# Four fp32 load buffers instead of five, and five fp16 split buffers instead of four, in a graph network kernel

## The reference

```python
def L0(x, adj):                 # passes 1 to 4
    h = relu(adj @ (f1[:, None] * (adj @ (x @ W1))))
    return adj @ (f2[:, None] * (adj @ (h @ W2)))
def L1(x, adj):                 # pass 5
    return concatenate([x, adj @ x], 1) @ weight
def L2(x, adj):                 # pass 6, the gated one
    m = x @ W_msg + b_msg
    gates = sigmoid((m @ W_q) @ (m @ W_k).T / sqrt(128) + gate_bias) * adj * adj
    return layernorm_affine(relu(concatenate([x, gates @ m], 1) @ W_upd + b_upd))
def L3(x, adj):                 # passes 7 and 8
    x1 = swish((adj @ x) @ W + b)
    return swish((adj @ x1) @ W + b)
x = layernorm(x + L(x, adj))    # for L in L0, L1, L2, L3
```

## Time and profile before

| what | value |
|---|---|
| median of 3 runs | 1719.76 us (1717.48 to 1719.78) |
| the profiled execution's own time | 1721.57 us |
| its span, first to last instruction | 1719.7 us |
| mean granted TensorE clock | 0.984 |
| TensorE matmul busy | 1627.4 us (95%) |
| VectorE busy | 1289.4 us (75%) |
| ScalarE busy | 1087.7 us (63%) |
| moved by DMA | 473.99 MB, 276 GB/s over the span |

### The profile page before, as it was taken

How to read it: one execution, slowest core, us unless ns; L and a number is a source line. 1 busy time by engine, 2 the same in 40 slices (tenths; PEclk the granted TensorE clock), 3 DMA queues, 4 the chain that set the end, 5 groups by cost and what they waited for, 6 DMA issues and landing times. The chain is left out here.

```text
span 1719.7 us, 18856 instructions
## 1 busy us (share of the span) xinstructions
PE 1627.4 (95%) x7618; PEld 763.6 (44%) x7618; DVE 1289.4 (75%) x1439; ACT 1087.7 (63%) x741; POOL 11.3 (1%) x25
## 2 busy tenths in 40 slices
PE   7999999999999999999999999898998799999996
PEld 4444444444444444444454444343434344444442
DVE  6875547554766497749996898989899996455997
ACT  5766747674664566456666786776768666445653
POOL 2000000000000000000000000000000000000000
PEclk9999999999999999999999999999999999999998
DMA  9989889987997788668686454444445797665992
GB/s 366 410 297 399 299 354 388 374 305 301 367 356 278 265 319 325 263 245 317 248 298 261 147 205 162 171 171 171 171 172 194 295 365 284 250 236 198 345 340 109
DMA packets 66120, 473.99 MB, mean 276 GB/s; under 512 B 7568, under 2 KB 7728, under 8 KB 9072
## 3 DMA queue, kind: packets, MB, share of 16 engines
q1 hardware_dynamic: 64800, 468.22, 72.0%
q0 software_dynamic: 1088, 4.49, 0.7%
q10 hardware_dynamic: 144, 0.07, 0.0%
HBM read 420.32 MB, written 52.43 MB: 275 GB/s over the span
## 5 line engine op out<-in xcount | busy, mean ns | idle before, releaser
L928 DVE SCALAR_TENSOR_TENSOR a_lo<-a_ring,a_hi 128x2048 f16<-128x2048 f32 x332 | 752.2, 2287 | 306.8 <-ACT a_hi L726 306.5
L726 ACT ACTIVATE a_hi<-a_ring 128x2048 f16<-128x2048 f32 x332 | 629.9, 1906 | 359.9 <-PE spare L548 217.5
L548 PE MATMUL acc<-a_hi,y_hi 128*128 128x512 f16 x1584 | 480.6, 385 | 54.2 <-DVE a_lo L928 34.3
L548 PE MATMUL acc<-a_hi,y_lo 128*128 128x512 f16 x1584 | 477.2, 382 | 0.0
L548 PE MATMUL acc<-a_lo,y_hi 128*128 128x512 f16 x1584 | 477.2, 382 | 0.0
L548 PEld LDWEIGHTS acc<-a_hi,y_hi 128*128 128x128 f16 x1584 | 153.6, 99 | 249.9 <-DVE a_lo L928 41.7
L548 PEld LDWEIGHTS acc<-a_lo,y_hi 128*128 128x128 f16 x1584 | 156.4, 99 | 192.7 <-issue 10.0
L548 PEld LDWEIGHTS acc<-a_hi,y_lo 128*128 128x128 f16 x1584 | 155.8, 98 | 190.3 <-issue 5.7
L962 DVE SCALAR_TENSOR_TENSOR gates<-gates,a_ring 128x1024 f32<-128x1024 f32 x128 | 155.8, 1218 | 28.4 <-ACT gates L761 27.4
L946 DVE TENSOR_TENSOR a_lo<-gates,a_hi 128x1024 f16<-128x1024 f32 x128 | 155.8, 1217 | 0.0
L740 ACT ACTIVATE a_hi<-gates 128x1024 f16<-128x1024 f32 x112 | 118.0, 1054 | 56.5 <-DVE gates L962 56.2
(11 more groups left out here) (100 smaller groups left out, 718.4 us busy)
## 6 DMA issues: line engine op xcount, KB each, us to landing
a_ring<-adj_dram SPq DMA_DIRECT2D x348, 1024.0 KB, 7.0
saved_squares<-squares SPq DMA_DIRECT2D x48, 1024.0 KB, 11.7
a_ring<-saved_squares SPq DMA_DIRECT2D x48, 1024.0 KB, 4.8
x_T<-xt_dram SPq DMA_DIRECT2D x4, 512.0 KB, 8.2
x_rows<-x_dram POOLq DMA_DIRECT2D x1, 2048.0 KB, 12.7
out_dram<-x_rows POOLq DMA_DIRECT2D x3, 512.0 KB, 4.1
out_dram<-x_rows SPq DMA_DIRECT2D x2, 256.0 KB, 2.0
w<-W_dram POOLq DMA_DIRECT2D x2, 64.0 KB, 5.4
```

What stands on the lines that cost most here:

```text
L548: mm = pe.matmul(sums[:, h * BANK:(h + 1) * BANK], blk(y[:, y_pass % 2, :], j), slot(a, st)[:, s, h * BANK:(h + 1) * BANK], start=(begins ...
L726: act.activation(slot(a_hi, st), loaded(st), ACT.Copy, scale=2.0 ** A_EXP).then_inc(s_ahi, 1)
L928: dve.scalar_tensor_tensor(out=slot(a_lo, st).rearrange("p s c -> p (s c)"), in0=loaded(st).rearrange("p s c -> p (s c)"), scalar=2.0 ** A ...
```

## The change

Two constants are exchanged. One load buffer and one slot of both split rings have 8 KiB in each partition, so the memory is the same. Nothing else is edited, but all code that uses the constants follows: the wait of each load, the slots, the wait of `a_hi`, the position of every epilogue piece of the plain passes on ScalarE and VectorE, and the wait of GpSimd's small loads.

```diff
-LOADS = 5
-RING = 4
+LOADS = 4
+RING = 5
```

## The result

The changed kernel takes 1739.2 us (median of 4 runs, 1737.5 to 1739.7) beside 1719.8 before: ratio 1.0104, 95% interval 1.0092 to 1.0116. It is slower, as forecast, but by 19.4 us where 8 were forecast, and it lies 2 us above the upper end of the range. The profiled execution spans 1735.7 us, 16.0 more than before; the traces account for these 16.0, and the 3.4 us to the medians' difference are not in them. The profiled execution was the fastest of the four (1737.5 us, mean granted clock 0.979); the other three had a clock of 0.976 or 0.977.

What follows compares the result with a forecast made beforehand. TensorE was taken as the bound, with VectorE in layer-norm stretches and loads from 50 to 75 us. Terms summed to +7.95 us, 1729.5 against the profiled 1721.57, hence a median of 1727.7 us; range 1714 to 1737.

Steps and rivals of the forecast that it cites:

- the first claim under buffering: Buffering sum stays nine, so with PE as the bound a load starts at the same moment; only splits move.
- the loads starve: Rival: four buffers give 2.9 us a step at a 7.4 us landing, 25 to 30 us slower, 1747; chance 0.1.
- start: PE's first wait for y_lo, chunk 1: it stands behind the fifth split, +2.5 us, bounds 0 and 4.2.
- pass 2, 280 us: z_T at 279.00 behind one more a_hi and square: +3.5 us, bounds 1.2 and 5.5.
- pass 3, 454 us: z_T behind one more split, loads lying ready, so 1.5 us won back: +2.1 us, bounds 1.0 and 3.6.
- pass 4, first norm: First layer norm: wait of 3.42 us shrinks, but z_T comes later; +1.5 us, bounds -2.7 and 3.2.
- pass 4, 704 us: Extra split fits before the norm, closing PE's 2.49 us gap and its clock fall: -4.2 us.
- pass 5: Gap at 777.61 closes, z_T near 804 stands behind one more load: +0.3 us net, bounds -4.2 and +4.
- pass 7: VectorE saturated, last y_lo behind one more split, first loads a gated step later: +2.0 us, bounds -1.75 and 3.3.
- pass 8: Last norm's 2.59 us gap closes, about 1 us lost at a swish: -1.5 us, bounds -4.3 and +1.
- clock: One clock fall more, net of new and closed PE gaps: +1.75 us, bounds -1.75 and 5.2.
- The bursts decide: Rival: extra splits done in VectorE's idle time, pieces not late, gains stand alone: 8.9 us faster, 1711; chance 0.16.

Runs made afterwards that it cites:

- four loads alone: Kernel before with LOADS = 4 in place of 5 and RING kept at 4: 1735.8 us, ratio 1.0086.
- the half loads: Changed kernel with each load after the first four, except the gated pass's, cut to its first 0.5 MiB: 1720.6 us, ratio 1.0002.
- the old places: Epilogue pieces placed among the splits as before the change (`freed` with RING = 4); the changed kernel with them: 1739.2 us, ratio 1.0104.
- the new places: Epilogue pieces placed one split later, as by `freed` with RING = 5; put alone into the kernel before (five loads, four slots): 1821.2 us, ratio 1.0579.
- five and five: Kernel before with five load buffers, five split slots, three square slots: 1725.1 us (1.0024) with new places, 1714.3 us (0.9958) with old places.
- the control: Kernel before with three slots for the squares in place of four, k's low part overwriting its high part: 1721.4 us, ratio 1.0000.

## Why the prediction was right in sign and wrong in size

**The step that failed** is the first claim under buffering, that with nine steps kept the lost load buffer costs nothing, together with the case against "the loads starve". That a load starts at the same moment did hold: the issue of each load, less TensorE's own shift at that time, moved by 0.0 us in the median of the 57 loads from 30 to 230 us and by 0.7 in the 48 from 230 to 440. But a split that is one slot further ahead wants its load one step sooner. From issue to that moment there were 5 x 2.6 - 4.2 = 8.8 us before and are 4 x 2.6 - 4.2 = 6.2 us now (an estimate from the step and the split), and the landing takes 6.6 us in the median. Between 258 and 275 us ScalarE does this in the kernel before, then in the changed one:

```profile
262.47 1.91 ACT L726 ACTIVATE a_hi<-a_ring 128x2048 f16<-128x2048 f32 x1 [0.68 <-PE acc L548]
265.06 1.91 ACT L726 ACTIVATE a_hi<-a_ring 128x2048 f16<-128x2048 f32 x1 [0.68 <-PE acc L548]
```

```profile
266.18 1.91 ACT L726 ACTIVATE a_hi<-a_ring 128x2048 f16<-128x2048 f32 x1 [1.23 <-DMA a_ring<-adj_dram]
269.92 1.91 ACT L726 ACTIVATE a_hi<-a_ring 128x2048 f16<-128x2048 f32 x1 [1.83 <-DMA a_ring<-adj_dram]
```

Before, the load lay ready and the split waited for its slot. In the changed kernel the slot is free and the load is not there. An extra slot is filled early only if its load lands early, and with four buffers it doesn't there. The forecast had said so of single places ("where the load has landed") and then took it as given in its sum.

The rival was dismissed on the word that with four buffers the landing should shrink toward 4.7 us, for a turn of 8.9 us or 2.2 a step. It shrank much less. Where the forecast had read 7.4 us, the changed kernel has 6.8 (from 1611 to 1631 us, the same place shifted by its delay). Tile `a_ring`, whole span, issue to landing, in the changed kernel:

```profile
DMA to landing us min/median/max: 4.6/6.6/16.7
```

The median was 6.8. A turn is 6.6 + 4.2 = 10.8 us, 2.7 a step, and TensorE wants 2.6. That is also the pace of the changed kernel's splits from 44 to 78 us: (75.6 - 43.1)/12 = 2.71 us, with a median landing of 6.5. In the dense stretch of pass 1, tile `a_ring` from 44 to 78 us, with four loads alone:

```profile
L928 DVE SCALAR_TENSOR_TENSOR a_lo<-a_ring,a_hi x13: 2291/2292/2293, 42.8 to 76.9; 128x2048 f16<-128x2048 f32 x13
...
DMA to landing us min/median/max: 6.4/7.2/7.5
```

(76.9 - 42.8)/12 = 2.84 us a step, and 4 x 2.84 = 11.4 = 7.2 + 4.2: the turn closes. The forecast's 5.7 us landing at 2.48 us a step would have needed the queue to stay full with fewer loads in it; at the lower depth the landing shrank from 8.1 to 7.2 only. That is the rival's mechanism with the rival's landing (7.4), and the half loads show it from the other side: with a median landing of 4.6, a turn of 8.8, the loss is gone. The section "Anatomy of one DMA" of the Trainium skill's page DMA: Bandwidth & Descriptors gives the time of one DMA issued by GpSimd, for 1 MiB an estimate of 4.4 us, near the 4.6 us of the fastest load here; the section "Bandwidth" has 6.15 us for 1 MB, as the time that the DMA engines are busy with one of GpSimd's. Both are of another queue than these loads, and the forecast's sentence on the second, that the starving would then just begin, was nearer: the median here is 6.6. Its 0 to 3 us were still too few.

The rival's size, 1747, was too large: its turn was 2.9 us a step and the measured one is 2.7, and in steps with an own and a next unit TensorE takes 5.2 us, in which loads can catch up (argued, not measured apart). The truth lies between it and the forecast, and its chance of 0.1 was too low.

**The gain was put down to the wrong effect.** The forecast has the bursts' gain under buffering: a fifth slot keeps one more split ready. The runs put it with the places. Waits of TensorE for plain splits with five slots and the old places, first with four load buffers, then with five:

```profile
PE acc L552 <- DVE a_lo L932: 39.9, 22, 5.2
```

```profile
PE acc L552 <- DVE a_lo L932: 32.9, 15, 5.2
```

Before it was 34.3 in 16 (of the 39.9, 4.9 are the six waits in pass 1). With the new places it is 16.0 in the change, 14.0 with five and five, and 27.0 in 10 even with four slots. The wait of 2.49 us at 706.88 is 2.50 with five and five and old places, and gone with the new places and four slots. By the program, a split that stands behind the norm is not done before it, whether a slot is free or not. So the gain before a norm and the loss before a z_T are two sides of one move. A kernel that puts only the norms one split later and leaves z_T and y_lo in their old places was not run; whether it keeps both is open.

**Step by step.** The start of the same instruction of TensorE, changed kernel less kernel before, gives each stretch its part. Beside it stands the same for five and five with new places: the places and the fifth slot when no load buffer is lost (and three square slots). The clock is in the measured columns.

| stretch | forecast | the change | five and five, new places |
|---|---|---|---|
| start | +2.5 | +5.3 | +4.2 |
| pass 2, 280 us | +3.5 | +6.0 | +3.4 |
| pass 3, 454 us | +2.1 | +2.8 | -0.6 |
| pass 4, first norm | +1.5 | +3.5 | +1.7 |
| pass 4, 704 us | -4.2 | -4.2 | -4.2 |
| pass 5 | +0.3 | +2.3 | -2.3 |
| gated pass | 0 | -1.0 | +1.0 |
| pass 7 | +2.0 | +4.1 | +0.5 |
| pass 8 | -1.5 | -2.6 | -2.7 |
| clock | +1.75 | in the rows | in the rows |
| sum | +7.95 | +16.2 | +1.0 |

The last column is one profiled execution (1720.6 us, near the low end of that kernel's 1719.4 to 1729.1); its median says +4 against the control, and the old places say that the new ones cost 11.

- Start: the place and the size of the step were right. y_lo goes behind the fifth split, and TensorE resumes at 26.45 us and not at 24.00, 2.45 later for 2.5 forecast. (The wait itself grew by 1.63 us only, as TensorE came to it 0.8 us later.) The other 2.8 us are lost behind the wait at the low clock, beyond the 1.75 of one fall: the bound of 4.2 was met by five and five and passed by the change.
- Pass 2: the wait grew by 4.14 - 0.86 = 3.28 us, forecast 3.5: a hit. The rest, 2.7 us, is clock, and with it the stretch passed its bound of 5.5. Stretches of the changed kernel (us, then busy (instructions) of PE, PEld, DVE, ACT and POOL, granted clock, DMA share, GB/s):

```profile
0.00:75.00 75.00, 61.94 (x283) 32.98 (x284) 52.12 (x25) 46.03 (x27) 9.14 (x21) 0.91 0.95 363
275.00:300.00 25.00, 20.86 (x92) 10.98 (x91) 13.45 (x8) 15.78 (x10) 0.00 (x0) 0.86 0.99 400
450.00:475.00 25.00, 21.26 (x90) 9.91 (x88) 16.78 (x9) 17.48 (x10) 0.00 (x0) 0.86 1.00 412
...
800.00:825.00 25.00, 18.58 (x89) 11.46 (x88) 17.71 (x9) 14.81 (x9) 0.00 (x0) 0.86 0.96 361
```

  The last three stretches of the kernel before had clocks of 1.00, 0.93 and 1.00. (Of its first 17 us no clock is on record, so the first can't be compared: its two matmuls from 13.90 us take 1.04 us together, and the same two take 1.03 in the changed kernel.) With a wait of 4.14, 3.74 or 6.42 us the stretch loses 0.14 x 25 = 3.5 us of full clock, twice the term that the forecast took from a wait of 2.36. Part of it falls into the wait itself: after it TensorE lost 2.7 us at 282 and 2.6 us at 804. This is the mis-sized term. The forecast's clock is nothing net, +1.75 in its own row and -1.75 in that of 704 us; by the page it costs 3.3 us.
- Pass 3: +2.8 for 2.1, inside its bounds; the wait is 3.74 us for 2.36. With five loads nothing is lost here.
- Pass 4: at the first norm 3.5 passed the bound of 3.2. The z_T for which TensorE waited 0.25 us costs it 5.43. Late loads are the smaller part of that: with five loads it is 4.46. The gain at 704 us came to within a tenth of a microsecond, in both columns: there the load had landed long before. Its size was right; its cause is the place and not the slot, as shown above.
- Pass 5: the gap at 777.61 closed, then z_T came 6.42 us late. VectorE does five splits in a row ahead of it, each behind a load; ScalarE's a_hi in the changed kernel:

```profile
795.63 1.91 ACT L726 ACTIVATE a_hi<-a_ring 128x2048 f16<-128x2048 f32 x1 [3.49 <-DMA a_ring<-adj_dram]
...
808.62 1.91 ACT L726 ACTIVATE a_hi<-a_ring 128x2048 f16<-128x2048 f32 x1 [1.95 <-DMA a_ring<-adj_dram]
...
813.59 1.91 ACT L726 ACTIVATE a_hi<-a_ring 128x2048 f16<-128x2048 f32 x1 [0.60 <-DMA a_ring<-adj_dram]
```

  The forecast had the mechanism and one load of 2.48 us; it was more than one. With five loads the same wait is 3.47 us.
- Gated pass: nothing of note, as forecast. Pass 7: +4.1 for 2.0, above the bound of 3.3; with five loads it is 0.5, so this too is the loads. Pass 8: all three waits before a norm, 2.59, 2.31 and the 2.59 of the earlier trace rows, are gone, but waits for z_T of 2.77 and 2.67 us and the 0.73 at 1711 are new; -2.6, inside the bounds.

Of the signs named beforehand, all those for "right" came (z_T waits near 4 us at 282 and 454 us, none at 704, a longer one near 804, half the time for `a_lo`), except that y_lo's wait was 2.98 and not 3.8. The sign named for "starving", ScalarE waiting for loads in many steps, came as well: 123 waits for 19. The forecast treated the two as exclusive, and both are there.

"The bursts decide" fell with z_T's waits. That the places and the loads are two costs, and that late loads hide the places, is shown by the table of kernels: with four whole loads the places are worth 0.0%, with halved loads 0.36%, with five loads 0.66%. Why a fifth slot with four loads and old places is no better than four slots (1.0104 and 1.0086, the intervals overlap) stays open. Whether half loads help by their shorter landing or by the bandwidth that they leave wasn't separated.

## What to carry to other kernels

Count load buffers by the turn they make, landing as measured in the running kernel plus the work that holds the buffer, divided by their number, and not by the landing of a load that stands alone; when that is within some tenths of a microsecond of the bound engine's step, as here (2.7 against 2.6), expect one buffer fewer to cost where a lead is needed. It is not enough that a load starts as early as before: ask also when it is wanted. Memory given from one ring to the next helped here only where the second ring could be filled sooner, and a rule that derives the place of urgent work from a ring's depth should be cut loose from it before the depth is changed. Look for the memory elsewhere first: a tile of other use that idles in those passes gave the slot here without taking a load buffer.

## What the runs showed of the hardware

Over the whole span the landing of a 1 MiB load hardly depends on the number of buffers (medians of 6.6 us with four, 6.8 with five), but in the dense stretch it goes 7.2, 8.1 and 10.8 us with four, five and six (old places, four slots), while the pace of the splits goes from 2.84 us to 2.5 and no further. The fastest load of 1 MiB lands after 4.6 to 4.7 us and the fastest of 0.5 MiB after 3.4; an estimate from the two is that about 2.1 us don't depend on the size.

The stretches with longer waits of TensorE have mostly more time at 1.2 GHz: the stretch with a wait of 2.36 us has a mean granted clock of 0.93, those with 3.74, 4.14 and 6.42 us have 0.86. But the order isn't strict: the stretch from 650 to 675 us, with the wait of 5.43, has 0.93, and with five and five the stretch at 450 us has a wait of 3.38 us and a clock of 1.00, so a wait alone doesn't decide it.
